# Reordering the SBUF tile allocations of a four-block transformer kernel so that every large tile begins at a multiple of 128 bytes

## The reference, cut to what matters

```python
x = x + tanh(g_xattn[0]) * L0_xattn(ctx, ctx, layernorm(x))   # A: cross attention, softmax over the heads
x = x + tanh(g_ffn[0])   * L0_ffn(layernorm(x))               # B: silu(x Wg) * (x Wu), then Wd, hidden 768
x = x + tanh(g_xattn[1]) * L1_xattn(layernorm(x), ctx)        # C: cross attention with one key/value head
x = x + tanh(g_ffn[1])   * L1_ffn(layernorm(x))               # D: one 256x256 product with a low-rank part
```

## The kernel before

| product | matmuls | moving tile | stationary tile |
|---|---|---|---|
| gate and up of block B (`gate_up`) | 72 | `xt_hi_B`, `xt_lo_B` | `w_hi`, `w_lo` |
| queries A (`queries`) | 12 | `xt_hi_A`, `xt_lo_A` | `w_hi`, `w_lo` |
| queries C | 12 | `xt_hi_C`, `xt_lo_C` | `w_hi`, `w_lo` |
| down of block B (`down`) | 36 | `w_hi`, `w_lo` | `h_hi`, `h_lo` |
| output A and output C (`rows_out`) | 12 each | `w_hi`, `w_lo` | `y_hi_A/C`, `y_lo_A/C` |
| block D (`rows_out`) | 12 | `w_hi`, `w_lo` | `xt_hi_D`, `xt_lo_D` |

## Time and profile before

### The profile page before, as it was taken

How to read it: one execution, slowest core, us unless ns; L and a number is a source line. 1 busy time by engine, 2 the same in 40 slices (tenths; PEclk the granted TensorE clock), 3 DMA queues, 4 the chain that set the end, 5 groups by cost and what they waited for, 6 DMA issues and landing times.

```text
span 2442.8 us, 70142 instructions
## 1 busy us (share of the span) xinstructions
PE 2357.7 (97%) x27814; PEld 2081.6 (85%) x27814; DVE 2205.6 (90%) x3678; ACT 1719.5 (70%) x3402; POOL 1773.4 (73%) x2512
## 2 busy tenths in 40 slices
PE   6899999999999999999999999999999999999897
PEld 5788888888888888888888888888888888888786
DVE  6879999999999999999999999999999999999963
ACT  4567777777777777777777777777777777777664
POOL 3667777777777777787777777777777777777653
PEclk9999999999999999999999999999999999999999
DMA  3000010010011010011001000001001001101000
GB/s 106 25 19 29 28 35 24 28 35 24 28 35 30 22 35 30 26 31 30 28 28 30 28 28 31 28 28 35 24 28 35 24 28 35 30 22 35 17 19 15
DMA packets 74326, 73.26 MB, mean 30 GB/s; under 512 B 6555, under 2 KB 73393, under 8 KB 74290
## 3 DMA queue, kind: packets, MB, share of 16 engines
q1 hardware_dynamic: 74290, 72.75, 9.5%
HBM read 54.90 MB, written 16.78 MB: 29 GB/s over the span
## 4 chain that ended last, share of the span: by engine, by line
PE 64%; DVE 19%; ACT 7%; POOL 7%; issue 2%; DMA 0%; POOLq 0%; SPq 0%; DVEq 0%; ACTq 0%
PE work L2136 13%; PE work L2137 11%; PE work L2138 11%; DVE m L1517 6%; PE scores L2229 6%; PE scores L2239 5%; PE work L2272 5%; PE work L2175 4%; DVE scores L1523 4%; ACT e L857 3%; POOL zt L417 3%; PE scores L2218 3%; ACT xn_D L814 3%; PE work L2153 2%; PE work L2159 2%
## 5 line engine op out<-in xcount | busy, mean ns | idle before, releaser
L857 ACT ACTIVATE e<-scores 120x1024 f32<-120x1024 f32 x512 | 513.4, 1029 | 88.3 <-PE scores L2239 56.6
L2136 PE MATMUL work<-xt_hi_B,w_hi 128*128 128x256 f32 x1536 | 456.5, 297 | 3.8 <-DVE y_lo_A L1497 1.6
L2137 PE MATMUL work<-xt_lo_B,w_hi 128*128 128x256 f32 x1536 | 430.2, 280 | 0.0
L2138 PE MATMUL work<-xt_hi_B,w_lo 128*128 128x256 f32 x1536 | 430.0, 280 | 0.0
L417 POOL TENSOR_TENSOR zt<-e 120x512 f32<-120x512 f32 x256 | 328.7, 1285 | 118.1 <-ACT e L857 112.1
L411 POOL TENSOR_TENSOR h_lo<-h_f,h_hi 128x256 fp32r<-128x256 f32 x384 | 279.5, 735 | 147.3 <-ACT h_hi L807 147.1
L1517 DVE TENSOR_REDUCE m<-scores 120x128 fp32r<-120x2048 f32 x128 | 291.0, 2273 | 66.2 <-PE scores L2229 66.0
L2136 PEld LDWEIGHTS work<-xt_hi_B,w_hi 128*128 128x128 f32 x1536 | 289.3, 188 | 60.6 <-DVE h_f L1511 24.9
L1523 DVE TENSOR_TENSOR scores<-scores,m 120x1024 f32<-120x1024 f32 x256 | 302.8, 1227 | 4.3
L1535 DVE TENSOR_TENSOR e<-e,work 120x2048 f32<-120x2048 f32 x128 | 291.4, 2277 | 0.2
L2137 PEld LDWEIGHTS work<-xt_lo_B,w_hi 128*128 128x128 f32 x1536 | 289.9, 189 | 0.0
(11 more groups left out here) (256 smaller groups left out, 7283.5 us busy)
## 6 DMA issues: line engine op xcount, KB each, us to landing
x_ln<-xp SPq DMA_DIRECT2D x64, 256.0 KB, 2.7
x_res<-xp SPq DMA_DIRECT2D x64, 256.0 KB, 2.7
y<-y_out SPq DMA_DIRECT2D x64, 256.0 KB, 2.2
ctx_f_A<-cp SPq DMA_DIRECT2D x64, 128.0 KB, 2.5
ctx_f_C<-cp SPq DMA_DIRECT2D x64, 128.0 KB, 2.0
qm<-mT SPq DMA_DIRECT2D x256, 4.0 KB
e<-wi SPq DMA_DIRECT2D x3, 768.0 KB, 5.5
w_ctx<-wc SPq DMA_DIRECT2D x1, 656.0 KB
```

The lines of the kernel that those rows point to most:

```text
L857: return act.activation(e[0:SC, c, 2 * h:2 * h + 2, :, :].rearrange("p a b n -> p (a b n)"), scores[0:SC, 2 * h:2 * h + 2, :].rearrange("p ...
L2136: pe.matmul(out, a_hi, b_hi_, start=first, stop=False, skip_group_check=parts)
L2137: pe.matmul(out, a_hi, b_lo_, start=False, stop=False, skip_group_check=parts)
L2138: last = pe.matmul(out, a_lo, b_hi_, start=False, stop=end, skip_group_check=parts)
```

## The change

The calls of `sb` are sorted into two groups: first every tile of 512 bytes or more per partition, in their old order, then every smaller tile (masks of parities, biases, layer-norm statistics, `v1_one`, `rz_q`, gates). The tile `masks`, which nothing reads, is dropped. No shape, slice, instruction or wait is changed; only line numbers shift by 7. The core of the diff:

```diff
         ident = sb("ident", [P, P])
-        masks = sb("masks", [P, 2])
         neg_ident = sb("neg_ident", [P, P], F32R)
         wk0 = sb("wk0", [P, KC * D])
-        parity = sb("parity", [P, 2])
-        row_of = sb("row_of", [P, 4])
-        neg_row = sb("neg_row", [P, 2])
         w_ctx = sb("w_ctx", [P, CCOLS])
         ones_k = sb("ones_k", [P, D], F32R)
-        bias_col = sb("bias_col", [P, 2 * KC])
-        key_bias = sb("key_bias", [P, 2, KC])
...
-        minus_half = sb("minus_half", [P, NT])
-        eps_tile = sb("eps_tile", [P, NT])
-        zero_tile = sb("zero_tile", [P, NT])
...
         xt_hi = {s: sb(f"xt_hi_{s}", [P, KC, S], F32R) for s in "ABCD"}
         xt_lo = {s: sb(f"xt_lo_{s}", [P, KC, S], F32R) for s in "ABCD"}
+        ctx_f = {s: sb(f"ctx_f_{s}", [P, KC, P]) for s in "AC"}
+        qt = {st: sb(f"qt_{st}", [P, KC * S]) for st in "A"}
...
+        h_hi = sb("h_hi", [P, HC, S], F32R)
+        h_lo = sb("h_lo", [P, HC, S], F32R)
+
+        parity = sb("parity", [P, 2])
+        row_of = sb("row_of", [P, 4])
...
         stats = {s: sb(f"stats_{s}", [P, NT, 6]) for s in "ABCD"}
...
-        v1_one = sb("v1_one", [P, 2 * HD])
...
+        tg = sb("tg", [P, 4])
+        graw = sb("graw", [P, 4])
```

More of the change, by code:

```diff
@@ L122, in flamingo_kernel @@
         xt_lo = {s: sb(f"xt_lo_{s}", [P, KC, S], F32R) for s in "ABCD"}
-        stats = {s: sb(f"stats_{s}", [P, NT, 6]) for s in "ABCD"}
-        mv = {s: sb(f"mv_{s}", [P, NT, 2]) for s in "ABCD"}
-        var_eps = {s: sb(f"var_eps_{s}", [P, NT]) for s in "ABCD"}
-        ln_count = sb("ln_count", [P, 1])
-        neg_mean = {s: sb(f"neg_mean_{s}", [P, NT]) for s in "ABCD"}
-        shift = {s: sb(f"shift_{s}", [P, NT]) for s in "ABCD"}
-        rstd = {s: sb(f"rstd_{s}", [P, NT]) for s in "ABCD"}
         ctx_f = {s: sb(f"ctx_f_{s}", [P, KC, P]) for s in "AC"}
@@ L150, in flamingo_kernel @@
         yz_q = sb("yz_q", [P, KC, 2, S // 32, 2 * HD])
-        rz_q = sb("rz_q", [P, KC, 2, S // 32])
         y_q = sb("y_q", [P, KC, S // 32, 2, HD])
         y1f = sb("y1f", [P, KC, S])
-        bias_row = y1f[0:1, :, :].rearrange("p k n -> p (k n)")
         y_hi = {s: sb(f"y_hi_{s}", [P, KC, S], F32R) for s in "AC"}
@@ L161, in flamingo_kernel @@
         h_lo = sb("h_lo", [P, HC, S], F32R)
+        parity = sb("parity", [P, 2])
+        row_of = sb("row_of", [P, 4])
+        neg_row = sb("neg_row", [P, 2])
+        bias_col = sb("bias_col", [P, 2 * KC])
+        key_bias = sb("key_bias", [P, 2, KC])
+        minus_half = sb("minus_half", [P, NT])
+        eps_tile = sb("eps_tile", [P, NT])
+        zero_tile = sb("zero_tile", [P, NT])
+        stats = {s: sb(f"stats_{s}", [P, NT, 6]) for s in "ABCD"}
+        mv = {s: sb(f"mv_{s}", [P, NT, 2]) for s in "ABCD"}
+        var_eps = {s: sb(f"var_eps_{s}", [P, NT]) for s in "ABCD"}
+        ln_count = sb("ln_count", [P, 1])
+        neg_mean = {s: sb(f"neg_mean_{s}", [P, NT]) for s in "ABCD"}
+        shift = {s: sb(f"shift_{s}", [P, NT]) for s in "ABCD"}
+        rstd = {s: sb(f"rstd_{s}", [P, NT]) for s in "ABCD"}
+        v1_one = sb("v1_one", [P, 2 * HD])
+        rz_q = sb("rz_q", [P, KC, 2, S // 32])
+        tg = sb("tg", [P, 4])
+        graw = sb("graw", [P, 4])
+        bias_row = y1f[0:1, :, :].rearrange("p k n -> p (k n)")
         e0_flat = e0[:, :, :, :, :].rearrange("p a b c d -> p (a b c d)")
@@ L174, in flamingo_kernel @@
         luT_s = e1_flat[0:4, small + 4 * D + 4:small + 4 * D + 54]
-        tg = sb("tg", [P, 4])
-        graw = sb("graw", [P, 4])
         scores = ctx.enter_context(nc.psum_tensor("scores", [P, 4, 512], F32))
```

## The result

The changed kernel takes 2454.27 us (median of 7 runs, 2449.72 to 2454.93); the kernel before took 2446.94 us (7 runs, 2443.48 to 2448.32) beside it. The ratio is 1.0026, with a 95% interval of 1.0016 to 1.0037: slower by about 6 to 7 us, a little more than the 0.2% that can be told from no change. The forecast was 2463, slower by 16.

What follows compares the result with a forecast made beforehand. PE bounds 24.7 us of each 36.30 us iteration; DVE, ACT and POOL carry 11.6. Slower products add 0.31 us, 19.6 over 64 sequences, 16 arriving: span 2442.8 + 16 = 2458.8, plus 4.1 gives 2463 us, range 2453 to 2470.

Steps and rivals of the forecast that it cites:

- the pitch of rows 6: keep_busy's time per matmul, about 120 ns with both operands at 0 (mod 128), taken for every product after the change.
- gate and up: On PE's part of the chain: 72 products going from 117.3 to 120 ns, 194 ns more per iteration.
- queries A: On PE's part of the chain: 12 products slower by 2.7 ns each, 32 ns more per iteration.
- output A: On PE's part of the chain: 12 products going from 113.3 to 120 ns, 80 ns more per iteration.
- block D: On PE's part of the chain: products already at 120 ns, so 0 ns change.
- Four fifths: Share of the 19.6 us expected to arrive, 16 us, the rest partly falling into PE's wait for `h_f`.
- The step from the span to the runs: Runs stand 4.1 us above the profiled span, taking the forecast from 2458.8 to 2463 us.
- Off the chain for nothing: Down, output C and queries C: 0.26 us more per iteration, free because below PE's 0.83 us wait for `xn_D`.
- Everything else at 0: Other engines, transfers and small tiles: no change, with 4 us either way over the run for the 11.6 us leg.
- Alignment helps: Rival: products reach 113.3 ns wherever both operands begin at multiples of 64 bytes; 2426 us, chance 0.29.
- Nothing moves: Rival: the time between products follows from something the edit keeps, or no address matters; 2447 us, chance 0.21.
- Slower than I say: Rival: products go beyond 120 ns, 6.9 us per nanosecond on 108 chain matmuls; one more gives 2470; no separate chance.

Runs made afterwards that it cites:

- e2: Changed kernel plus one unused tile of 64 bytes before `x_ln`: 2434.84 us, ratio 0.9956 to the kernel before.
- e6: Changed kernel plus one unused tile of 128 bytes before `x_ln`, a repeat run: 2459.08 us, ratio 1.0050 to the kernel before.
- e1: Changed kernel plus unused 32-byte tiles before `x_ln` and before `ctx_f`, small tiles left at the end: 2449.53 us, ratio 1.0008 to the kernel before.
- e7: Changed kernel plus 64 unused bytes before `h_hi`, so only `h_hi` and `h_lo` move: 2452.96 us, ratio 1.0018 to the kernel before.
- e9: Changed kernel plus 64 unused bytes before `x_ln` and 128 before `xt_hi_D`, stationary meant 64 ahead of moving everywhere: 2436.29 us, ratio 0.9960 to before.
- e8: Changed kernel plus 192 unused bytes before `x_ln`, operands 64 apart with the other sign: 2442.57 us, ratio 0.9981 to the kernel before.
- e3: Changed kernel plus one unused tile of 32 bytes before `x_ln`: 2451.91 us, ratio 1.0020 to the kernel before.
- e5: Changed kernel plus 64 unused bytes before `w_hi`, moving all large tiles together: 2453.90 us, ratio 1.0024 to the kernel before.

## Why the prediction was right in direction and wrong in size

**The direction, and where it acts: right.** In the profiled iterations PE's part of the chain carries the whole difference: 24.49 us in e2, 24.68 before, 24.78 after, 24.85 in e6, and 11.62 for the leg in all four. The size per run follows the iteration, within 3 us in every kernel: 64 x (36.106 - 36.308) = -12.9 us for e2, whose median is 13.2 under before; 64 x 0.180 = +11.5 for e6, whose median is 11.5 over it; 64 x 0.092 = +5.9 after, +7.3 by the medians; the farthest is e1, +4.3 and +1.5.

**The step that failed: "Moving and stationary operand of every product then stand as those of keep_busy do ... and I take the pitch of rows 6, 120 ns, for all of them".** I counted modulo 128, and there they do. Modulo 256 the weights stay at 128 and `xt`, `y` and `h` come to 0: they are 128 apart, while keep_busy reads the weights on both sides. e6, where they really are 0 apart, shows the forecast state and gives 2459 us. At 128 the pitches are lower:

- gate and up, 72 x (118.5 - 117.4) = 79 ns, forecast 194
- queries A, 12 x 0.4 = 5 ns, forecast 32
- output A, 12 x (119.2 - 113.4) = 70 ns, forecast 80
- block D, 12 x (118.7 - 120.0) = -16 ns, forecast 0

That is 0.14 us per iteration for the forecast 0.31, and gate and up, the largest term, is most of the miss.

**"Four fifths" of it, for the wait for `h_f`: a share without a ground.** That wait was 25.2, 25.2, 25.2 and 25.1 us before, after, in e2 and in e6. What arrives is less than the sum all the same: 92 of 138 ns after, 202 of 268 in e2 (the sum over the same four terms), 180 of 251 in e6. Most of the gap is in the way of counting, the forecast's as well as mine above: it takes the pitch times all 72 or 12 products, but a stretch has one step less than products, and its first steps are not at the pitch. From first to last start of each stretch on the chain, over the same 51 iterations, gate and up got longer by 56 ns after, output A by 44 and queries A by 5, and block D shorter by 14: 91 ns together. By the same measure e2 is 243 ns shorter and e6 179 longer. A second part is a wait. PE's wait for ScalarE's exponentials ahead of L2239 took 15.3 us before, 14.5 after, 13.5 in e6 and 17.8 in e2, which is -13, -28 and +39 ns per iteration. It gives way in both directions; for e2 it is the second row here:

```profile
PEld work L2169 <- ACT xn_D L808: 51.6, 60, 1.2
...
PEld scores L2233 <- ACT e L851: 17.8, 63, 2.5
```

The changed kernel has 14.5 in the third row of its waits above. With both, 78 ns of the 92 are found after, -204 of the -202 in e2 and 151 of the 180 in e6. The rest, up to 29 ns, lies in the plain float32 matmuls between the stretches and the steps into them, and has no cause shown.

**The step from the span to the runs: 4.1 us, in part luck.** The profiled executions last about 2.4 us longer than their spans (2454.06 against 2451.7 after). So the profiled execution before took some 2445.2 us, an estimate, and the other 1.7 us are its distance from the median.

**Off the chain for nothing: right.** Down, output C and queries C went into the wait for `xn_D`, 0.83 to 0.68 us per iteration, and e7 changed down alone without an effect on the time.

**Everything else at 0: right.** ScalarE and GpSimd's rows above stayed within 1%, VectorE was busy as long as before, the leg stayed at 11.62 us in four kernels with different remainders, and in e1 the products account for the whole difference with the small tiles moved.

**The rivals.** "Alignment helps" fell: at remainder 0 nothing settles at 113. One piece of it holds, that the 120 ns of keep_busy belong to operands at the same place, and e6 shows that it needs no shared bytes. "Nothing moves" fell with e2 against e6: 64 or 128 unused bytes before `x_ln` and nothing else, 2434.8 or 2459.1 us. Of the two pages of the Trainium skill that it leaned on, "TensorE: Matmul & The Clock Gate", part "Step-by-step: what each phase is for", says that loading the next weights takes no read bandwidth from the running matmul. The runs do not bear out what the prediction drew from it: from one product to the next it is 113 to 120 ns by the distance between the two tiles. Whether it is read bandwidth that is short, no run shows. "SBUF — State Buffer", section "Who interferes with whom", says that PE waits on nobody, in a list of what engines do to each other; since PE's own two operands make the difference here, the runs say nothing against that. "Slower than I say" asked for more than 120 ns; the highest loop mean in any kernel is 120.2. The pitch of 120 in the forecast was right for operands at the same place; these operands were not there.

## What to carry to other kernels

When float32r products bound a kernel, look at the start addresses of the moving and the stationary tile of each pair, and try 64, 128 and 192 unused bytes ahead of one of the two groups: here the best (64) and the worst (128) are 1% apart. Aligning all tiles alike is the wrong aim, since it brings operands to the same place or half a period from it. Before taking a duration from a row of the same instruction, ask what the row's operands have in common that yours will not, and to what modulus that was checked. And where a difference of a few us is at stake, compare executions at the same granted clock.

## What the runs showed of the hardware

- The time from one float32r product of 128x256 to the next, with loads of weights between, was 120.0 ns in block D with 0 or +96 bytes (modulo 256) between the operands, 117.3 to 119.5 in gate and up with -96, 128 or 0, about 118 to 119 at 48 and 80, and 113.3 or 117.7 at 64. Why one of the two at 64 is open: neither sign (e9) nor address (two stretches of e8) nor the place in the program (output A of e9, 23 stretches at one and 41 at the other) decides it. At -96 queries A have two values too, 117.3 before and 118.7 in e3.
- 128 bytes more change it (e6 against the changed kernel, 119.5 for 118.5 and about 5 us), so the period is more than 128. 256 bytes more change nothing at the one pair of distances where the kernels allow it (before against e3: 117.4 and 117.3 ns, 120.0 twice).
- The distance counts and not the start itself: all tiles moved together by 64 bytes give the same pitches within 0.2 ns (e5).
- ScalarE's and GpSimd's rows and the leg of VectorE did not react to any of the placements read here (rows within 1%, 11.62 us in four kernels).
- One kernel takes 5 us more at a mean granted clock of 0.994 than at 0.997 (2449.7 and 2444.7 us for the kernel before).
